# The finish of the last image pair: products on the vector engine, centring and variance in two PSUM banks, three output tiles with a bank each, stores by tile

## What is computed

```python
y = out_y[:, 0] + inv_y[:, 0] + wh_y + invwh_y        # four scan directions, 192 channels
mu = y.mean(-1, keepdims=True)
var = y.var(-1, keepdims=True)
y = (y - mu) / jnp.sqrt(var + 1e-05) * out_norm_g + out_norm_b
y = y * jax.nn.silu(z)
x1 + y @ out_proj_w.T                                 # x1: output of the first stage
```

## Time and profile before

| | us |
|---|---|
| median of 3 runs | 3151.25 (3150.14 to 3152.01) |
| the profiled execution | 3149.67 |
| its span in the profile | 3147.9 |
| outside the span | 1.77 |
| PE busy in the span | 2729.5 |
| DVE busy | 2614.6 |
| POOL busy | 2136.7 |
| ACT busy | 1804.4 |

### The profile page before, as it was taken

How to read it: one execution, slowest core, us unless ns; L and a number is a source line. 1 busy time by engine, 2 the same in 40 slices (tenths; PEclk the granted TensorE clock), 3 DMA queues, 4 the chain that set the end, 5 groups by cost and what they waited for, 6 DMA issues and landing times.

```text
span 3147.9 us, 100459 instructions
## 1 busy us (share of the span) xinstructions
PE 2729.5 (87%) x39088; PEld 2032.2 (65%) x39088; DVE 2614.6 (83%) x4163; ACT 1804.4 (57%) x3808; POOL 2136.7 (68%) x1814
## 2 busy tenths in 40 slices
PE   4999999998896788888888888888888888888886
PEld 3999999996554556565656566665665656656554
DVE  6444444445887999999999999999999999999985
ACT  1111111111225777777777777777777777777764
POOL 5333333330005889889898898988988889888883
PEclk9999999999997999999999999999999999999999
DMA  5000000002334555555555555455554555545541
GB/s 205 0 0 0 0 0 0 0 0 77 129 127 147 157 160 161 166 157 161 167 151 163 161 156 180 142 170 163 149 177 144 175 166 147 168 144 173 178 125 48
DMA packets 57086, 385.30 MB, mean 122 GB/s; under 512 B 10100, under 2 KB 15060, under 8 KB 31700
## 3 DMA queue, kind: packets, MB, share of 16 engines
q1 hardware_dynamic: 57044, 384.79, 39.2%
HBM read 352.64 MB, written 32.11 MB: 122 GB/s over the span
## 4 chain that ended last, share of the span: by engine, by line
POOL 35%; issue 29%; PE 23%; DVE 9%; ACT 2%; POOLq 1%; DMA 0%; ACTq 0%; DVEq 0%; SPq 0%
POOL arena L495 23%; PE ps L1107 10%; PE ps L1116 10%; POOL arena L468 3%; POOL arena L477 3%; POOL arena L482 3%; POOL arena L472 3%; DVE arena L788 2%; DVE arena L785 2%; PE ps L1103 2%; DVE conv_out L203 2%; POOL arena L460 1%; DVE stats L571 1%; DVE stats L710 1%; POOL arena L455 1%
## 5 line engine op out<-in xcount | busy, mean ns | idle before, releaser
L1239 PE MATMUL ps<-arena,ident 128*128 128x392 f32 (+1 forms) x4096 | 1163.3, 417 | 0.9 <-DVE arena L797 0.9
L963 ACT ACTIVATE ps<-arena,abias,a 128x390 f32<-128x390 f32 x1024 | 689.0, 677 | 315.5 <-DVE arena L788 177.7
L1239 PEld LDWEIGHTS ps<-arena,ident 128*128 128x128 f32 x4096 | 683.0, 191 | 144.1 <-DVE arena L797 1.2
L797 DVE TENSOR_TENSOR arena<-arena,ps 128x784 f32<-128x784 f32 x768 | 745.5, 971 | 27.5 <-PE ps L1229 1.2
L785 DVE TENSOR_TENSOR_SCAN arena<-ps,arena 128x392 f32<-128x392 f32 x768 | 702.7, 956 | 22.8 <-POOL arena L495 22.3
L788 DVE TENSOR_TENSOR_SCAN arena<-ps,arena 128x392 f32<-128x392 f32 x768 | 702.6, 956 | 0.0
L1229 PE MATMUL ps<-arena,sel 96*128 96x196 bf16 x3072 | 392.2, 250 | 319.4 <-DVE arena L797 319.3
L1229 PEld LDWEIGHTS ps<-arena,sel 96*128 96x128 bf16 x3072 | 230.3, 98 | 624.4 <-DVE arena L797 592.2
L495 POOL TENSOR_TENSOR arena<-arena 128x784 f32<-128x784 f32 x256 | 473.9, 1851 | 129.0 <-PE ps L1239 126.6
L967 ACT ACTIVATE ps<-arena,abias,a 128x195 f32<-128x195 f32 x1024 | 474.8, 504 | 138.9 <-DVE arena L785 71.9
L495 POOL TENSOR_TENSOR arena<-arena,wh_sb 128x784 f32<-128x784 f32 x256 | 471.8, 1849 | 69.1 <-PE ps L1239 66.7
(11 more groups left out here) (176 smaller groups left out, 3013.2 us busy)
## 6 DMA issues: line engine op xcount, KB each, us to landing
wx_sb<-b_by_state SPq DMA_DIRECT2D x64, 1568.0 KB, 6.3
wh_sb<-b_by_state SPq DMA_DIRECT2D x64, 1568.0 KB, 6.2
arena<-b_by_image SPq DMA_DIRECT2D x128, 784.0 KB, 9.0
arena<-x_seq SPq DMA_DIRECT2D x4, 2352.0 KB, 15.9
x_in<-x_pair SPq DMA_DIRECT2D x16, 588.0 KB, 4.3
x_dram<-x SPq DMA_DIRECT2D x16, 588.0 KB, 3.1
x<-x_dram SPq DMA_DIRECT2D x16, 588.0 KB, 10.0
out<-xhat SPq DMA_DIRECT2D x16, 588.0 KB, 2.9
```

Source lines behind the costliest of these rows:

```text
L797: dve.tensor_tensor(h, h, bank(3), ALU.mult).then_inc(s["readout_ready"], 1)
L963: ins = act.activation(r, src, ACT.Exp, scale=a01[:, c:c + 1], bias=abias01[:, c:c + 1])
L1239: mm = pe.matmul(ps[:, 5 if g < 8 else 6, 0:cols], ident[:, :], h[:, m * cols:(m + 1) * cols], start=(opens and m == 0), stop=(closes and ...
```

## The change

Only the finish of the last pair is rewritten, and one slot of the last pair.

- **PE, slot (3, 10) of the last pair**: the centring products of `y_hw` for part 0, in bank 7, are issued here, three matmuls behind `reduce`.
- **PE behind the last pair**: bank 0 is opened with `x1` (tile 0 times identity) after the last scan and ahead of the last `reduce`. Part 1 of centring and variance goes to bank 3 and no longer waits for bank 7 to be read. Banks 1 and 2 are opened with tiles 1 and 2 of `x1` behind the centring and the variance. The projection accumulates onto the opened banks: the three products with columns 0 to 391 of `yc` once part 0 is gated, then the six with columns 392 to 587.
- **ACT**: each part of `yc` is squared as soon as it is copied, and each part of the logarithm is followed by its exponential. `affine` is left out there.
- **DVE** takes over the two products and the affine step in four `scalar_tensor_tensor` instructions, two for each part: `(yc * g) * rs` and `(that + b) * z_fin`. POOL has none of it for the last pair.
- **SP**: three DMAs of one tile each, each issued when its tile is ready.

```diff
--- before.py
+++ after.py
@@ -366,8 +366,10 @@
             with nc.Fori(1, PAIRS - 1, engines=[sp.engine], hint_back_edge=True) as i:
                 pair(i, False, False)
             pair(PAIRS - 1, False, True)
-            store(PAIRS - 1)
-            sp.wait_ge(s["out_stored"], 16 * PAIRS)
+            for oc in range(KC):
+                sp.wait_ge(s["o_ready"], (PAIRS - 1) * 3 + oc + 1)
+                sp.dma_start(out[PAIRS - 1][:, oc * T2:(oc + 1) * T2], o_sb[:, oc, :]).then_inc(s["out_stored"], 16)
+            sp.wait_ge(s["out_stored"], 16 * (PAIRS - 1 + KC))
 
 
         @block.gpsimd
@@ -536,8 +538,6 @@
             with nc.Fori(1, PAIRS - 1, engines=[pool.engine], hint_back_edge=True) as i:
                 pair(i, False, False)
             pair(PAIRS - 1, False, True)
-            normed(PAIRS - 1)
-            gated(PAIRS - 1)
 
 
         @block.vector
@@ -809,6 +809,16 @@
                 pair(i, False, False)
             pair(PAIRS - 1, False, True)
 
+            END = PAIRS - 1
+            dve.wait_ge(s["fin_z"], PAIRS * 16)
+            for part, (lo, hi, table) in enumerate(((0, T2, par01), (T2, TC, par2))):
+                dve.wait_ge(s["rstd2_step"], END * 3 + 2 * part + 2)
+                dve.scalar_tensor_tensor(y_hw[:, lo:hi], yc[:, lo:hi], table[:, P_G:P_G + 1], rs[:, lo:hi], ALU.mult, ALU.mult
+                                         ).then_inc(s["norm_step"], 1)
+                dve.wait_ge(s["norm_step"], END + part + 1)
+                dve.scalar_tensor_tensor(yc[:, lo:hi], y_hw[:, lo:hi], table[:, P_B:P_B + 1], z_fin[:, lo:hi], ALU.add, ALU.mult
+                                         ).then_inc(s["gated"], 1)
+
 
         @block.scalar
         def _(act):
@@ -978,11 +988,11 @@
                         src = src.rearrange("p (r w h) -> p r h w", w=W, h=H)
                     act.activation(dst, src, ACT.Copy).then_inc(s["y_drained"], 1)
 
-            def centred(i, part):
+            def centred(i, part, bank=7):
 
                 act.wait_ge(s["centred"], i * 2 + (part + 1))
                 lo, hi = ((0, T2), (T2, TC))[part]
-                act.activation(yc[:, lo:hi], ps[:, 7, 0:hi - lo], ACT.Copy).then_inc(s["yc_ready"], 1)
+                act.activation(yc[:, lo:hi], ps[:, bank, 0:hi - lo], ACT.Copy).then_inc(s["yc_ready"], 1)
 
             def square(i):
 
@@ -996,16 +1006,16 @@
                     act.activation(ysq[:, lo:hi], ysq[:, lo:hi], ACT.Identity, scale=table[:, P_G:P_G + 1], bias=table[:, P_B:P_B + 1]
                                    ).then_inc(s["affine_done"], 1)
 
-            def result(i, oc):
+            def result(i, oc, bank=7):
 
                 act.wait_ge(s["oproj_ready"], i * 3 + (oc + 1))
-                act.activation(o_sb[:, oc, :], ps[:, 7, 0:T2], ACT.Copy).then_inc(s["o_ready"], 1)
-
-            def log_var(i, part):
+                act.activation(o_sb[:, oc, :], ps[:, bank, 0:T2], ACT.Copy).then_inc(s["o_ready"], 1)
+
+            def log_var(i, part, bank=7):
 
                 act.wait_ge(s["var_ready"], i * 2 + (part + 1))
                 lo, hi = ((0, T2), (T2, TC))[part]
-                act.activation(rs[:, lo:hi], ps[:, 7, 0:hi - lo], ACT.Ln, bias=EPS).then_inc(s["rstd2_step"], 1)
+                act.activation(rs[:, lo:hi], ps[:, bank, 0:hi - lo], ACT.Ln, bias=EPS).then_inc(s["rstd2_step"], 1)
 
             def rstd(i):
 
@@ -1072,16 +1082,19 @@
             with nc.Fori(1, PAIRS - 1, engines=[act.engine], hint_back_edge=True) as i:
                 pair(i, False, False)
             pair(PAIRS - 1, False, True)
-            drain(PAIRS - 1, True)
-            for part in range(2):
-                centred(PAIRS - 1, part)
-            square(PAIRS - 1)
-            for part in range(2):
-                log_var(PAIRS - 1, part)
-            rstd(PAIRS - 1)
-            affine(PAIRS - 1)
+            END = PAIRS - 1
+            halves = ((0, T2), (T2, TC))
+            drain(END, True)
+            for part, (lo, hi) in enumerate(halves):
+                centred(END, part, (7, 3)[part])
+                act.wait_ge(s["yc_ready"], END * 2 + part + 1)
+                act.activation(ysq[:, lo:hi], yc[:, lo:hi], ACT.Square).then_inc(s["ysq_ready"], 1)
+            for part, (lo, hi) in enumerate(halves):
+                log_var(END, part, (7, 3)[part])
+                act.wait_ge(s["rstd2_step"], END * 3 + 2 * part + 1)
+                act.activation(rs[:, lo:hi], rs[:, lo:hi], ACT.Exp, scale=-0.5).then_inc(s["rstd2_step"], 1)
             for oc in range(KC):
-                result(PAIRS - 1, oc)
+                result(END, oc, oc)
 
 
         @block.tensor
@@ -1245,19 +1258,19 @@
                 pe.matmul(ps[:, 5, 0:T2], skip01[:, :], xc[:, 0:T2], start=False, stop=False)
                 pe.matmul(ps[:, 6, 0:T], skip2[:, :], xc[:, T2:TC], start=False, stop=False).then_inc(s["skipped"], 1)
 
-            def over_channels(weights, parts, part, done, opens=True, closes=True):
+            def over_channels(weights, parts, part, done, opens=True, closes=True, bank=7):
 
                 mm = None
                 for src in parts:
                     first, last = opens and src is parts[0], closes and src is parts[-1]
                     if part == 0:
-                        pe.matmul(ps[:, 7, 0:T2], weights[:, 0, :], src[:, 0:T2], start=first, stop=False)
-                        pe.matmul(ps[:, 7, 0:T], weights[:, 1, :], src[:, T2:TC], start=False, stop=False)
-                        mm = pe.matmul(ps[:, 7, T:T2], weights[:, 2, :], src[:, T2:TC], start=False, stop=last)
+                        pe.matmul(ps[:, bank, 0:T2], weights[:, 0, :], src[:, 0:T2], start=first, stop=False)
+                        pe.matmul(ps[:, bank, 0:T], weights[:, 1, :], src[:, T2:TC], start=False, stop=False)
+                        mm = pe.matmul(ps[:, bank, T:T2], weights[:, 2, :], src[:, T2:TC], start=False, stop=last)
                     else:
-                        pe.matmul(ps[:, 7, 0:T], weights[:, 3, :], src[:, T2:TC], start=first, stop=False)
-                        pe.matmul(ps[:, 7, 0:T], weights[:, 4, :], src[:, 0:T], start=False, stop=False)
-                        mm = pe.matmul(ps[:, 7, 0:T], weights[:, 5, :], src[:, T:T2], start=False, stop=last)
+                        pe.matmul(ps[:, bank, 0:T], weights[:, 3, :], src[:, T2:TC], start=first, stop=False)
+                        pe.matmul(ps[:, bank, 0:T], weights[:, 4, :], src[:, 0:T], start=False, stop=False)
+                        mm = pe.matmul(ps[:, bank, 0:T], weights[:, 5, :], src[:, T:T2], start=False, stop=last)
                 if closes:
                     mm.then_inc(done, 1)
 
@@ -1347,6 +1360,10 @@
                             bc_proj(i if st < 2 else i + 1, KS[(st + 2) % K4], g - 8)
                         if (st, g) == (0, 10):
                             skip()
+                        if last and (st, g) == (3, 10):
+                            pe.wait_ge(s["o_ready"], i * 3)
+                            pe.wait_ge(s["y_drained"], i * 4 + 2)
+                            over_channels(centring, (y_hw,), 0, s["centred"], closes=False)
 
             pe.wait_ge(s["bcw_step"], 13)
             pe.wait_ge(s["sel_step"], 13)
@@ -1368,19 +1385,34 @@
             with nc.Fori(1, PAIRS - 1, engines=[pe.engine], hint_back_edge=True) as i:
                 pair(i, False, False)
             pair(PAIRS - 1, False, True)
+            END = PAIRS - 1
+
+            def open_with_x1(oc):
+                pe.matmul(ps[:, oc, 0:T2], ident[:, :], x1[:, oc, :], start=True, stop=False)
+
+            pe.wait_ge(s["fin_x1"], PAIRS * 16)
+            pe.wait_ge(s["scan_done"], PAIRS * K4 * GRP * 2)
+            open_with_x1(0)
             pe.wait_ge(s["readout_ready"], PAIRS * K4 * GRP)
             reduce(K4 - 1, GRP - 1)
-            centre_hw(PAIRS - 1)
-            centre_wh()
-            centre_rest(PAIRS - 1)
-            pe.wait_ge(s["yc_ready"], 2 * PAIRS)
+            over_channels(centring, (y_hw,), 1, s["centred"], closes=False, bank=3)
+            pe.wait_ge(s["y_drained"], PAIRS * 4)
+            over_channels(centring, (y_wh,), 0, s["centred"], opens=False)
+            over_channels(centring, (y_wh,), 1, s["centred"], opens=False, bank=3)
+            open_with_x1(1)
+            pe.wait_ge(s["ysq_ready"], END + 2)
             for part in range(2):
-                var(PAIRS - 1, part)
+                over_channels(avg, (ysq,), part, s["var_ready"], bank=(7, 3)[part])
+            open_with_x1(2)
+            pe.wait_ge(s["gated"], END + 1)
             for oc in range(KC):
-                if oc == 0:
-                    pe.wait_ge(s["rstd2_step"], 3 * PAIRS)
-                out_proj(PAIRS - 1, oc)
-                residual(PAIRS - 1, oc)
+                pe.matmul(ps[:, oc, 0:T2], wout01[:, oc * 128:(oc + 1) * 128], yc[:, 0:T2], start=False, stop=False)
+            pe.wait_ge(s["gated"], END + 2)
```

(5 more changed lines are left out.)

## The result

The changed kernel took 3135.6 us in the median of five runs (3128.8 to 3137.07), the kernel before 3150.22 beside it (3150.12 to 3152.01). The ratio is 0.9947, 95% interval 0.9933 to 0.9962. It is faster by 14.6 us by the medians, and by 16.7 by the ratio, which goes with the means and so with one short execution of 3128.8 us. A second set of five runs of the same kernel gave 3137.85 against 3151.36, ratio 0.9957 (0.9943 to 0.9971), 13.5 us by the medians. The forecast was 3136.7 in 3134.4 to 3140.5.

A forecast was written before the change was run, and what follows sets the result against it. DVE sets the pace to the last read-out, then a 29.6 us chain of waiting engines. Savings 3.41 + 1.85 + 2.84 + 5.69 + 0.69 = 14.5 us; 3151.25 - 14.5 = 3136.7 us, range 3134.4 to 3140.5.

The forecast's parts named there:

- The sum: From the last read-out's start to the end of the span: 3.41 + 1.85 + 2.84 + 5.69 + 0.69 = 14.5 us less.
- All six steps: From last read-out to span end: drain 3.43, centring 3.60, variance 2.74, products 1.42, projection 4.69, store 2.62 us.
- moved centring: PE, slot (3, 10): the spread starts 0.3 us later but has 0.9 us of cover; costs nothing, bounds 0 to 0.3.
- opening of bank 0: PE ahead of the last sum: costs nothing, bounds 0 to 0.3 us; x1 lands 1.9 us before it is needed.
- The store's landing: Last tile's 196 KB store lands 2.2 us after issue, bounds 2.0 and 2.9; store step 2.62 us instead of 3.31.
- the centring: Centring, copies and squares behind the last drain, to the start of the variance: 3.60 us instead of 7.01.
- The vector products: DVE ahead of the projection: 0.62 us per product of 392 columns, bounds 0.41 and 0.97; step 1.42 instead of 4.26.
- The clock: TensorE in the projection: full clock, since PE idles about 1 us at most and had borne 1.24 us idle.
- the runs lie within 1 us of their median: Scatter term of the whole time: 1 us, used with the price bounds to give 3134.5 to 3139.5 us.
- The fall of the clock: Rival: the clock falls at the wait for the gate; projection 2 to 4 us longer, 3140.7 at most; chance 0.08.
- the late `x1`: Rival: x1 landing beyond 6.7 us delays the last sum, 3140.0 us, chance 0.06; landing 22.7 us: 3152.7 us, chance 0.02.
- The lesser overlap: Rival: DVE's four instructions cost 0.97 us each and the parts don't run side by side; 3138.9 us, chance 0.14.

The follow-up runs named there:

- products alone: Kernel before with only the last pair's two products and affine step moved to four vector instructions; ratio 0.9997 (0.9988 to 1.0006), 3145.86 to 3153.31 us.
- products on POOL: Changed kernel with the two products back on POOL over all 588 columns and the affine step on ACT between them; 3137.38 us.
- one output bank: Changed kernel with the three output tiles one after the other in bank 7, x1 added behind each; 3142.53 us.

## Why the prediction was right or wrong

**The sum held.** Forecast 14.5 us less in the tail, measured 14.9. All six steps came within 0.3 us. The medians of the two sets of runs, 14.6 and 13.5 us apart, agree with it. The moved centring and the opening of bank 0 cost nothing, as argued from 0.9 us of cover and 1.9 us of slack; the trace shows the last sum at 1.02 us behind the read-out's start, and undoing the move costs 1.25.

**Two terms were mis-sized.** The store's landing was put at 2.2 and took 1.9, below the 2.0 that I had named as its bound: a store of 196 KB is faster than the line through 294 and 588 KB says, although the second tile's is still on its way when the third is issued. Why was not looked into. And the centring took 3.39 us and not 3.60, half by each of two hand-overs: PE started the variance 0.05 us behind the second square and not 0.15, and ACT started the second copy at 3114.99, 0.07 us before its first square had ended, where I had put it 0.04 behind. The copy does not depend on that square; the 0.04 was read from two instructions of which one needs the other. The vector products took 0.63, 0.63, 0.42 and 0.42 (forecast 0.62 and 0.42), so the row of the convolution's tap was the right one to take, and not the estimate of 0.57 by the Trainium skill (VectorE: DVE Perf Modes, section on the TRN2 errata), whose formula is for another instruction.

**The clock** stayed at 2.4 GHz, as forecast from the 1.24 us of idle time that it had borne; PE's longest idle time behind the drain was 0.89 us. The experiments with longer idle time (3.4 and 4.4 us) both show it at 0.50 in the projection, at 1.7 to 2 us, which is the price that the rival named for its lower end. The margin was narrower than the 5.4 us of the earlier trace rows suggest: the fall came 1.4 us into the idle time in one of them.

**The step that failed is "the runs lie within 1 us of their median".** It was read off three runs that happened to lie within 1.9 us of each other. Over 35 runs the kernel before lay between 3147.4 and 3153.1, and the changed kernel over ten between 3128.8 and 3138.6. So the term for the scatter, 1 us, had to be about 4 for the kernel before (3151.36 less 3147.42) and 6 to 7 for the changed one (3135.6 less 3128.8, 3137.85 less 3131.77). The range was also added up wrongly: 3136.7 less 0.5 of prices and 1 of scatter is 3135.2, where the prediction writes 3134.5 and then 3134.4; its upper end, 3140.5, is below the 3140.7 of its own rival. The median of the first five, 3135.6, lies in the range, but the ratio's 0.9947 times 3150.22 is 3133.5, below it, and two of the five runs (3128.8 and 3133.01) are below it too. It is a matter of one execution: without the profiled 3128.8 the means give a ratio of 0.9952, or 3135.0 us, which is inside. That execution has the short form of the recurrent stage (669.3 us), and the profile that the sum started from the long one (675.4); the sum itself, of differences in the tail, is not touched by that.

**The parts**, each undone by itself, cost 5.2 (products, with the clock), 4.6 (output banks), 1.85 (bank 3), 1.25 (slot (3, 10)) and 1.0 (stores), 13.9 together. The tail lost 14.9, so 1.0 is left for what was not undone alone, as the halves of square and exponential, and for what the parts do to each other; such costs need not add up. The products alone won 1.8 to 2.0 where their removal cost 5.2. Of the difference 1.7 is the clock; the rest goes with part 0 running ahead of part 1, which the removal took away too (POOL waits for both exponentials), and that split was not measured by itself.

**The rivals.** The fall of the clock and the late `x1` did not come. The lesser overlap did not either: DVE's third and fourth product lie beside PE's matmuls (3119.91 to 3122.15). No step of the chain got slower by more than 0.02 us.

## What to carry to other kernels

A finish that nothing hides is a chain; write it down from hand-over to hand-over, price each step by a row, and the sum is good to a few tenths of a microsecond. Give it more banks and halves so that every engine works on one half while the next takes the other, and pull what needs no late data (the residual, the first operand's products) ahead into slots where the engine waits. But measure such a change at a mark in the trace, not by the whole time alone: here the executions of one kernel differ by up to 10 us, more than any one part of the change is worth. And take the range of a forecast from more runs than three.

## What was not expected of the hardware

- The same kernel ran the same 196 recurrent steps, with PE busy throughout, in 675.4 us in one execution and 669.3 in another.
- A prefetch hint at the back edge of PE's loop made the slow step of each iteration longer (3.67 us, where it was 3.56 in the mean of the shorter executions and 3.61 in the longer ones) and the executions more alike.
- DVE stood idle for 5.7 to 7.8 us once, at the same group of the last pair in each of seven profiles, in five of them with nothing in the profile that it waited for.
- The clock fell to 0.50 about 1.4 us (vector products alone), 2.3 and 3.0 us (before, two profiles) and 5.2 us (products on POOL) behind the last matmul, and did not fall in 2.38 us of idle time (one output bank). With the products on POOL it fell while PE was already working again.
- A store of 196 KB landed in 1.9 us, one of 588 KB in 2.9.
